# Counting edges in strips of 12 rows instead of windows of 25, and the first norm's moments on ScalarE

## What is computed

```python
x = x + gnn(layernorm(x))       # h = relu(x @ W1 + b1) @ W2 + b2 ; h + segment_sum(h[dst], src)
x = x + ffn(layernorm(x))       # 8 experts of 512x512, weighted per token by a gated softmax
out = x
```

## Time and profile before

| | us |
|---|---|
| median of 3 runs (369.87 to 371.19) | 369.93 |
| profiled execution | 369.96 |
| its span, first to last instruction | 368.2 |
| PE busy | 351.1 (95%) |
| VectorE busy | 314.0 (85%) |
| ScalarE busy | 127.9 (35%) |
| VectorE compares (L771), 125 of them, busy | 91.0 |
| PE counting matmuls (L1108), 402, as recorded | 53.7 |
| PE hidden layer (L1056), 80 matmuls in the ten slots, as recorded | 19.6 |
| PE bias times deviation (L1058), 20, as recorded | 6.1 |
| PE aggregation (L1070), as recorded | 49.3 |
| ScalarE places (L493), 50 | 35.7 |

### The profile page before, as it was taken

How to read it: one execution, slowest core, us unless ns; L and a number is a source line. 1 busy time by engine, 2 the same in 40 slices (tenths; PEclk the granted TensorE clock), 3 DMA queues, 4 the chain that set the end, 5 groups by cost and what they waited for, 6 DMA issues and landing times.

```text
span 368.2 us, 7339 instructions
## 1 busy us (share of the span) xinstructions
PE 351.1 (95%) x2542; PEld 269.7 (73%) x2542; DVE 314.0 (85%) x565; ACT 127.9 (35%) x224; POOL 56.2 (15%) x83
## 2 busy tenths in 40 slices
PE   2999999999999989999999999999999999999995
PEld 1777787656656645457767888888888888888884
DVE  6799997999999878898686888889888888888764
ACT  5844354655679502377731313003030030210000
POOL 7000000000000000063632313050140500500000
PEclk9999999999999999999999999999999999999999
DMA  8971010222222250003000003030030300000133
GB/s 223 214 239 39 16 42 29 74 68 76 79 74 78 84 170 6 0 2 121 3 0 2 0 6 112 0 116 2 1 116 2 114 2 1 2 2 0 44 119 121
DMA packets 16273, 22.06 MB, mean 60 GB/s; under 512 B 2188, under 2 KB 9235, under 8 KB 16236
## 3 DMA queue, kind: packets, MB, share of 16 engines
q1 hardware_dynamic: 15820, 21.05, 19.4%
q10 hardware_dynamic: 416, 0.53, 0.6%
HBM read 12.77 MB, written 2.56 MB: 42 GB/s over the span
## 4 chain that ended last, share of the span: by engine, by line
PE 81%; DVE 10%; issue 3%; DMA 2%; DVEq 2%; ACT 1%; ACTq 0%
PE ps_g L1220 10%; PE ps_g L1221 10%; PE ps_g L1222 10%; PE ps_w L1108 9%; PE ps_g L1070 9%; DVE split L771 3%; PE ps_g L1056 3%; PE ps_a L1220 2%; PE ps_a L1222 2%; PE ps_a L1221 2%; PE ps_w L1221 2%; PE ps_w L1222 2%; PE ps_w L1220 2%; PE ps_g L1146 2%; DVE x_sb L854 2%
## 5 line engine op out<-in xcount | busy, mean ns | idle before, releaser
L771 DVE TENSOR_TENSOR split<-places,keys 125x1536 f16<-125x1536 int16 (+2 forms) x125 | 91.0, 794 | 4.3 <-PE ps_w L1108 1.9
L944 DVE SCALAR_TENSOR_TENSOR x_sb<-ps_g,weight_s,x_sb 125x256 f32<-125x256 f32 (+1 forms) x142 | 75.1, 546 | 19.6 <-PE ps_g L1222 18.4
L1220 PE MATMUL ps_g<-wb_hi,places 128*128 128x256 f16 x212 | 57.8, 273 | 0.1
L1221 PE MATMUL ps_g<-wb_lo,places 128*128 128x256 f16 x212 | 57.8, 273 | 0.0
L1222 PE MATMUL ps_g<-wb_hi,r_sb 128*128 128x256 f16 x212 | 57.8, 273 | 0.0
L1108 PE MATMUL ps_w<-split 125*128 125x250 f16 x402 | 53.7, 270 | 2.4 <-DVE split L771 1.8
L1108 PEld LDWEIGHTS ps_w<-split 125*128 125x128 f16 x402 | 36.7, 97 | 21.0 <-DVE split L771 8.4
L1070 PE MATMUL ps_g<-late,r_sb 125*128 125x512 f32 (+3 forms) x120 | 49.3, 516 | 1.7 <-DMA late<-counts 1.7
L574 ACT ACTIVATE wb_hi<-stage 128x512 f16<-128x512 f32 x7 | 4.4, 628 | 99.1 <-PE ps_g L1222 48.8
L1220 PE MATMUL ps_g<-wb_hi,split 128*128 128x256 f16 x142 | 38.7, 273 | 0.0
L1222 PE MATMUL ps_g<-wb_hi,split 128*128 128x256 f16 x142 | 38.7, 273 | 0.0
(11 more groups left out here) (223 smaller groups left out, 665.5 us busy)
## 6 DMA issues: line engine op xcount, KB each, us to landing
stage<-in_L_ffn_W_exp_dram SPq DMA_DIRECT2D x8, 1024.0 KB, 6.0
late<-counts SPq DMA_DIRECT2D x50, 122.1 KB
x_sb<-in_x_dram SPq DMA_DIRECT2D x5, 448.0 KB, 10.3
out_dram<-x_sb SPq DMA_DIRECT2D x10, 224.0 KB
w_sb<-in_L_gnn_W_dram SPq DMA_DIRECT2D x2, 512.0 KB, 10.0
out_dram<-x_sb ACTq DMA_DIRECT2D x10, 26.0 KB
b_sb<-in_L_gnn_b_dram SPq DMA_DIRECT2D x1, 250.0 KB
x_sb<-in_x_dram ACTq DMA_DIRECT2D x1, 208.0 KB
```

Of the source, the lines that this page charges most:

```text
L771: nc.vector.tensor_tensor(hot[hot_at(w, p)][:, 0:n, :].rearrange("p c (k x j) -> p (c k) x j", k=SEGS, j=2), places[w % WPT][:, 0:n, :].re ...
L944: nc.vector.scalar_tensor_tensor(out=x_sb[:, i, a:z], in0=bank[0:R, at:at + z - a], scalar=weight_s[:, expert_of(u), i:i + 1], in1=x_sb[:, ...
L1220: nc.tensor.matmul(out_cols, hi_x, wb_hi[par][:, q, k, :], start=(opens and k == 0), stop=False, skip_group_check=True)
L1221: nc.tensor.matmul(out_cols, hi_x, wb_lo[par][:, q, k, :], start=False, stop=False, skip_group_check=True)
```

## The change

Rows are counted in strips of 12. A strip's position is 10 x row + upper part of `src`, the lower part is below 125: 120 and 125 places, and a chunk's one-hots are two segments of 126 elements. Two strips make a group with one beginning: the second strip reads the chunks `behind` further on. The first two groups and the last hold one strip. There are 54 groups for 50 windows. A group's two strips share one PSUM bank (2 x 125 columns) and one eviction. All groups have four stages of two one-hot buffers with 6 chunks each. The places of all strips lie in one table of ascending numbers, written once in 19 pieces: five by ScalarE ahead of the keys, the rest one behind each eviction from group 7 on, and a compare reads two stretches of it (`places_of`). The table of words is worked out on one row, with constants for each group, on VectorE. VectorE no longer runs `statistics` of the first norm; ScalarE makes each tile's mean and mean square with two passes that sum their output (`moments`), four tiles ahead of the slots. Each strip is moved by a DMA of its own, two where it crosses into the next tile.

```diff
-    WIN = 25
-    HI = 5
-    LO = 250
+    WIN = 12
+    HI = 10
+    LO = 125
...
-    STEPS = ((1, (4, 4, 4, 4)), (2, (3, 3, 3, 3)), (4, (4, 4, 4, 4)), (6, (4, 4, 4)), (9, (4, 3, 3)), (18, (4, 4)),
-             (30, (3, 3)), (NW, (3, 2)))
-    FIXED = ((1, 2), (2, 1), (NW, 0))
...
+    FIXED = ((1, 2, (6, 6)), (2, 1, (4, 4)))
+    LOOP = ((1, (5, 5), 0), (2, (4, 4), 0), (3, (6,), 11), (4, (5,), 9), (5, (4,), 7), (10, (6,), 5), (13, (5,), 4),
+            (30, (4,), 3), (NG - 1, (3,), 2), (NG, (2,), 0))
...
+        def windows_of(g):
+
+            return (2 * g,) if g in (0, 1, NG - 1) else (2 * g, 2 * g + 1)
+
+        def row_of(v):
+
+            return WIN * (v // 2) if v < 4 else WIN * (v - 2)
...
-                sp.dma_start(a_t[i % 3][q * WIN:(q + 1) * WIN, :].rearrange("p (h l) -> p h l", h=HI),
-                             counts[q][0:WIN * HI, :]).then_inc(win_moved[q], 16)
...
+                for s, a, z, tile, at in MOVES[g]:
+                    if tile > begun:
+                        begun = tile
+                        sp.wait_ge(g_done, tile - 2)
+                        sp.wait_ge(a_summed, max(tile - 3, 1))
+                    sp.dma_start(a_t[tile % 3][at:at + z - a, :].rearrange("p (h l) -> p h l", h=HI),
+                                 counts[q][SHIFT + a * HI:SHIFT + z * HI, s * LO:(s + 1) * LO]).then_inc(win_moved[q], 16)
...
-            def deviations(j):
-                act.wait_ge(ln1_mv, 2 * j + 2)
-                nc.scalar.activation(std1[:, 2 * j:2 * j + 2], mv1[:, 2 * j:2 * j + 2, 1], ACT.Sqrt, bias=eps[0:R, :],
-                                     scale=1.0).then_inc(ln1_std, 1)
+            def moments(i):
+                act.wait_ge(x_in[i // 2], 16)
+                act.wait_ge(x_rest[min(i // 2, 1)], 16)
+                nc.scalar.activation(moment_out[:, :], x_sb[:, i, :], ACT.Copy, scale=-1.0 / D,
+                                     accum_out=minus_mean1[:, i:i + 1]).then_inc(ln1_mean, 1)
+                act.wait_ge(ln1_mean, i + 1)
+                nc.scalar.activation(moment_out[:, :], x_sb[:, i, :], ACT.Square, bias=minus_mean1[:, i:i + 1], scale=1.0,
+                                     accum_out=squares1[:, i:i + 1]).then_inc(ln1_squares, 1)
+                act.wait_ge(ln1_squares, i + 1)
+                nc.scalar.activation(std1[:, i:i + 1], squares1[:, i:i + 1], ACT.Sqrt, bias=eps[0:R, :], scale=1.0 / D).then_inc(ln1_std, 1)
...
-                if w + WPT < NW:
-                    positions(w + WPT)
...
+            def table(k):
+                a, z = k * PIECE, min((k + 1) * PIECE, TABLE)
+                nc.scalar.activation(places_all[:, a:z], places_all[:, 0:z - a], ACT.Identity, bias=piece_base[:, k:k + 1],
+                                     scale=1.0).then_inc(places_ready, 1)
...
+            for i in range(MOMENTS_AHEAD):
+                moments(i)
             turned(2)
             turned(3)
             for k in range(SLOTS):
-                if k in STD_AT:
-                    deviations(STD_AT[k])
+                if k + MOMENTS_AHEAD < TILES:
+                    moments(k + MOMENTS_AHEAD)
                 spread(k)
...
+            def places_of(v, n):
+
+                base = places_all[0:EP, 0:SEG]
+                return bass.AP(base.tensor, base.offset, [list(base.ap[0]), [0, n], [row_of(v) * HI, SEGS], [2, SEG // 2], [1, 2]])
...
+                        if p == 0:
+                            dve.wait_ge(hot_used, dve.snap(need_reg))
+                        nc.vector.tensor_tensor(hot[hot_at(stage, p)][:, 0:n, :].rearrange("p c (k x j) -> p c k x j", k=SEGS, j=2),
+                                                places_of(windows[s], n),
+                                                keys[:, ds(key_at, n * REC)].rearrange("p (c k j) -> p c k j", k=SEGS, j=2).unsqueeze(3)
+                                                .broadcast_to([EP, n, SEGS, SEG // 2, 2]),
+                                                ALU.is_equal).then_inc(hot_ready[p], 1)
...
-            SUM_AT = {4: T1, 5: T3, 6: T2, 7: T4}
+            SUM_AT = {5: T1, 6: T3, 7: T2, 8: T4}
+            COLUMNS_AT = {LAST[i] + SUM_LAG: i for i in range(1, TILES - 2)}
...
-                            mm = nc.tensor.matmul(bank[:, 0:LO], hot[hot_at(w, p)][:, c, 0:SEG], hot[hot_at(w, p)][:, c, SEG:SEG + LO],
+                            mm = nc.tensor.matmul(bank[:, s * LO:(s + 1) * LO], one_hots[:, c, HOT - 128:HOT], one_hots[:, c, 0:LO],
                                                   start=False, stop=False, skip_group_check=True)
-                        mm.then_inc(hot_used[p], 1)
+                    mm.then_inc(hot_used, 1)
```

More of the change, by code:

```diff
@@ L185, in gnn_moe @@
         a_sum = late[0:R, 3 * SW:4 * SW]
+        below, above, hit = (late[0:ROWS, k * GJ * NV:(k + 1) * GJ * NV].rearrange("p (j v) -> p j v", j=GJ) for k in range(3))
+        hit_idx = late[0:ROWS, 3 * GJ * NV:5 * GJ * NV].rearrange("p (a j v) -> p a j v", a=2, j=GJ)
         assert KD * N <= 4 * SW
@@ new lines, in compare, with one_step @@
+                dve.wait_ge(places_ready, 1 + table_part(g))
+                if g == 0:
+                    dve.wait_ge(pads_ready, 2)
+                windows = windows_of(g)
+                def one_step(stage, parts, k, ahead):
+                    for p, (s, n) in enumerate(parts):
+                        key_at = nc.s_assert_within(
+                            k + (s * behind_of(g) + sum(m for r, m in parts[:p] if r == s) - ahead) * REC, 0, (CHUNKS - n) * REC,
+                            skip_runtime_bounds_check_because="the table's steps begin at or behind a group's first chunk, the pads hold the rest")
+                        if p == 0:
[4 more added lines that the diff above has]
+                                                .broadcast_to([EP, n, SEGS, SEG // 2, 2]),
@@ L1120, in _ @@
-            for w in range(NW):
-                count(w)
-                if w < WPT + LAG:
-                    nc.tensor.matmul(ps_w[w % 2][:, 0:2], zeros[0:1, 0:128], zeros[0:1, 0:2], start=False, stop=True,
+                stage = stage_of(g)
+                steps, parts = fixed_of(g)
+                for f in range(steps):
+                    one_step(stage, parts)
+                    stage = stage + 1
+                    next_slot()
+                with pe.Fori(0, pe.value_load(wtab[0:1, NG + g:NG + g + 1])):
+                    one_step(stage, loop_of(g))
@@ new lines, in _ @@
+            pe.wait_ge(self_ready, 4)
+            begins = [LAST[i] + LAG for i in range(TILES)]
+            pieces = {}
+            for i in range(TILES - 1):
+                for n in range(len(cuts)):
+                    pieces.setdefault(begins[i] + min(n, 4), []).append((i, n))
+            for g in range(NG):
+                count(g)
+                if g not in pieces:
+                    nc.tensor.matmul(ps_w[g % 2][:, 0:2], zeros[0:1, 0:128], zeros[0:1, 0:2], start=False, stop=True,
```

488 lines of the change are left out of this document (247 added, 241 removed).

## The result

| | before | changed |
|---|---|---|
| median of the runs, us | 370.06 (4 runs, 369.87 to 371.19) | 389.24 (4 runs, 388.43 to 389.89) |
| ratio, 95% interval | | 1.0511 (1.0478 to 1.0543) |
| profiled execution and its span, us | 369.96, 368.2 | 389.89, 388.1 |
| start of the last column sum (T), us | 138.08 | 152.47 |
| degrees on VectorE, us | 142.18 | 160.31 |

The forecast was 367.8 us with a range of 362 to 377. The time lies 12 us above the range, on the other side of before.

What follows compares the result with a forecast made beforehand. VectorE's loop turn, 1.45 us a group, was taken to lead: from 63.3, 65.8 us end the compares at 129.1; a 6.8 us tail gives T 135.9, 2.2 us earlier than before: 367.8 us, range 362 to 377.

Steps and rivals of the forecast that it cites:

- The issue price of a strip's DMA: SyncE's queue: 0.62 us an issue, bounds 0.29 and 0.742; 101 issues from group 7 end at 130.0, behind VectorE.
- VectorE's turn of 1.45 us: Late groups on VectorE: sequencer steps and word load pace each at 1.45 us, 1.29 without waits; the forecast's case, chance 0.38.
- rival (a): SyncE's issue leads if an issue costs above 0.66 us: 372.1 us at 0.70, 376.4 at 0.742; chance 0.27.
- VectorE now runs four groups ahead: Early part: VectorE leads by four groups instead of two windows, through row 240 instead of 200, when slots end.
- ScalarE's ring: Early slots: bias, transpose, latency, copy, moments and spread take 4.1 us a slot after a first spread ended at 26.7.
- rival (c): ScalarE's accumulating passes cost 0.2 to 0.3 us more each, 4.5 us in all: 372 us; chance 0.10.
- rival (b): VectorE's sequencer load falls to its floor and TensorE leads, T near 131 to 133: 363 to 365 us; chance 0.17.
- TensorE's sum: TensorE from group 7 on: counting, own entries, aggregation, zero matmuls and seams, 65 us for 47 groups, 1.38 each.
- Counting matmuls: TensorE: 402 of 250 columns at 0.107 us become 476 of 125 at 0.06, bounds 0.057 and 0.107.
- rival (d): TensorE does not hide weight loads in counting: 371 us at 0.081 a matmul, 380 at 0.107; chance 0.08.
- The start: VectorE's preparation and table: first compare at 16.4 us instead of 13.68.
- The landing: Last strip's DMA: landing falls from 5.90 us to 3 or so with half the bytes, at 133.5, behind VectorE.

Runs made afterwards that it cites:

- The probes: Two sets of 16 extra DMAs of different shapes and memories, issued by SyncE in the kernel before; only issue times were read, 324 to 841 ns.
- the fastest variant: Changed kernel with last strips on GpSimd's queue from group 2, second turns of groups 2 to 4 unrolled, first-norm statistics on VectorE: 358.84 us, 0.9715 of before.
- the kernel before with two queues: Kernel before with two of five windows' strips issued by GpSimd instead of SyncE: 369.72 us, 1.0001 of before.
- unrolled: Changed kernel with the first turns of groups 2, 3 and 4 as fixed steps with their own buffer stage: 383.87 us, 5.4 less.
- the variants: Follow-up kernels: changed kernel with edits such as a second DMA queue, unrolled second turns or first-norm statistics on VectorE; 358.84 to 383.87 us.
- the run with GpSimd's queue: Changed kernel with the last strip of each group from group 2 on moved by a GpSimd DMA: 371.22 us, 1.0039 of before.

## Why the prediction was wrong, step by step

**The issue price of a strip's DMA: this step decides it.** The prediction said "I take 0.62", "nearer to the row of the same line, with part of the excess over 0.317 going with the shape". It is 0.772, above even the upper bound of 0.742. Both ends of the bound were badly chosen: the lower one came from DMAs that have one side in DRAM, and for 0.742 as a ceiling the only reason given is "half the bytes, other counts". The probes show that bytes hardly enter (0.798 for a fifth of them against 0.838), and three DMAs a window show it in the kernel itself (0.690 for a third). With that term too small the forecast let VectorE's turn of 1.45 us lead and put T at 135.9; in its place SyncE's queue led, and T was 152.5. The rule of decision in rival (a) was right, "above c = 0.66" SyncE leads; it had a chance of 0.27 only. It is the mechanism that the last line of the prediction names as its refutation: SyncE issuing without a gap from 63 us on, and the last column sum waiting for a landing.

**Why rival (a) at its upper bound still said only 376.** Its T was 144.5, measured 152.5. The gapless run began 4.6 us later than the 62.8 taken, its 101 issues took 83.5 us (67.4 to 150.9), 4.0 more than at 0.742 + 0.045, and T came 1.6 us behind it instead of 2.2: together the 8.0 us. And nothing in the sum stood for the clock: at the lower level 3.7 us more stand between T and the degrees, and 1.8 behind them (where the fastest variant, at the full clock, has 225.8 us and the kernel before 226.0). Forecast 367.8, T later by 16.6 than the 135.9 forecast, 3.7 and 1.8 for the clock: 389.9, the profiled execution's time taken apart. That the waits brought the clock down is argued from their order in time, not tested. In the profile of the kernel before it stayed up behind a wait of 5.90 us, in that of the kernel before with two queues it fell for 3.4 us at 142.9.

**"VectorE now runs four groups ahead": wrong.** It runs four stages ahead, and the second turn of a two-turn group reuses the first turn's stage. I had the number of turns from the counts and didn't carry it into the waits. It made the slots 5.5 us later (unrolled: 5.4 us of time alone, 5.7 with two queues).

**ScalarE's ring: the mechanism and its size were right.** First spread ended at 26.07 (forecast 26.7; 24.4 in the variants, whose first compare comes on time), 3.9 us a slot (4.1). The tile's passes, with the reading of the sum as an operation of its own:

```profile
15.79 0.62 ACT L532 ACTIVATE moment_out<-x_sb 125x512 f16<-125x512 f32 x1
16.31 0.19 ACT L532 ACTIVATION_READ_ACCUMULATOR moment_out<-x_sb 125x1 f32 x1
16.54 0.72 ACT L535 ACTIVATE moment_out<-x_sb,minus_mean 125x512 f16<-125x512 f32 x1
```

A tile takes 1.79 us against the 2.0 taken, the two readings included, so rival (c) did not come. What I missed is what the ring cost in time: 5.9 to 6.7 us by the runs without it. I had booked it as "gives nothing" and so as no loss.

**VectorE's work and its turn.** Compares busy 73.0 us (forecast 73.2). The turn of a late group was put at 1.45; where nothing holds VectorE's sequencer it is 1.21 (behind the column sum at 108.03 the loads of four groups begin at 109.90, 111.11, 112.31 and 113.53). The load of the next word now takes 0.309 at the median:

```profile
L833 DVEq TENSOR_LOAD <-wtab x56: 297/309/371, 20.0 to 138.0; - x56
```

It is 0.31 from 62 us on in the kernel before with three DMAs a window too, whose compares are the old ones, against 0.494 in the same stretch of the kernel before:

```profile
L788 DVEq TENSOR_LOAD <-wtab x40: 305/314/526, 62.9 to 144.3; - x40
```

So the new compares are not what the price needs to fall. That is rival (b)'s condition. It was met, and was worth nothing while SyncE led. With two queues and the early part mended TensorE leads, as (b) has it, so the sequencer is not the floor that the forecast took it for. But a group takes 1.49 us from group 7 on (46 in 68.8 us), not the 1.38 of TensorE's sum: that sum was too small by about 5 us.

**Counting matmuls: right.** Twelve of 125 columns go in 0.66 us, 0.055 each (forecast 0.06), so rival (d) fell. The 81 ns that the Trainium skill, page "TensorE: Matmul & The Clock Gate", section "Back-to-back issue gap", gives for pairs at 128 columns don't appear at this shape:

```profile
62.91 0.66 PE ps_w L1167 x12
```

**The start.** First compare 18.13 us, forecast 16.4. In this one execution VectorE's first operation on the edges' `dst` began at 4.80 us, in the profiles of the variants at 3.0 to 3.3, with the same code ahead of it. The fastest variant's first compare begins at 16.44, so the forecast of the start holds. Of the 1.6 us 0.7 are left at group 7's eviction (67.00 against 66.32 in the run with GpSimd's queue, which has the same code up to there), and so in the profiled T.

**The landing.** Forecast 3 us behind the issue "with half the bytes", measured 1.96 from its start, against 5.90 in the earlier trace rows. The direction is right and the reason is not: the last strip is two rows, 9.8 KB for a window's 122.1, which the forecast did not say.

```profile
late<-counts SPq DMA_DIRECT2D x1, 9.8 KB
```

What whole strips do is seen on GpSimd's queue: 2.8 us from issue to landing at the median in the fastest variant, 3.5 for whole windows in the kernel before.

Taken together, each by the runs that add or remove it: the strips with everything mended are worth 10 to 11 us (ratio 0.9715 against 1.0001 with a second queue on both), SyncE's count of DMAs costs 17 to 18, the two-turn groups 5.5, the moments on ScalarE 6 to 7. Minus 10 to 11 plus 28 to 30.5 is 17 to 20, for the 19 us measured.

## What to carry to other kernels

When a change splits transfers, multiply the issuing queue's price by the new count before anything else, and compare it with the pace of the engines: 101 x 0.815 = 82 us for the DMAs from group 7 on, against a stretch of some 70 us, decides this case in one line. Take the price from a row of the same kind (same memories, same cut of rows), and don't let it fall with bytes. If a queue leads, a second queue is a remedy, and what hides behind it (here a ring on ScalarE and buffers freed a turn too late) shows only once it is gone. And before a stretch is made cheaper for one engine, its next one has to be summed with its waits: here TensorE held the late stretch at 68.8 us where it had taken 68.5.

## What the hardware showed that I had not expected

- An issue of an on-chip copy costs 0.56 to 0.84 us on SyncE for 2 to 125 rows (second round of the probes). The strips cost 0.772 us on SyncE's queue, 0.572 on GpSimd's and 0.782 on ScalarE's; the windows of 25 rows cost GpSimd 0.766, no less than SyncE.
- A plain copy of 120 rows of 125 costs 0.419 us to issue from DRAM and 0.841 from on-chip memory.
- TensorE, busy for 4.43 of the 7 us to 151, was granted 0.50 from 151.2 to 164.7, and its 20 degree columns took 4.00 us for 2.09. The lost clock is over a quarter of the loss (5.5 of 19.9 us of span).
- The load of a table word by VectorE's sequencer fell from 0.414 to 0.309 us at the median, without an edit to it, and to 0.314 with the old compares once SyncE led. Its cause was not tested.
